# A four-layer attention and feed-forward kernel on one core: projections chunk by chunk in the opening, kept copies behind the linear features, weight splits grouped

## The chip, the cores and the metric

One core of one Trainium2 chip. A time is device microseconds (us) of one execution. Engines: TensorE (PE, with its weight loads PEld), VectorE (DVE), ScalarE (ACT), GpSimd (POOL) and SyncE (SP), which here only issues DMAs. Each engine works through its own list in order; semaphores make one wait for another.

## The reference

`x` is [2, 1024, 128] in float32. Eight sublayers follow, each as `x = x + layernorm(f(layernorm(x)))`:

```python
f0 = causal softmax attention, 16 heads of 8, rotary q and k      # softmax(rope(q) rope(k)^T / sqrt(8)) v, then W_o
f1 = x + 0.5 * mlp(layernorm(x))                                  # 128 -> 512 silu -> 128, dequantised weights
f2 = gated attention: sigmoid(s - mu) * exp(s), normalised        # no mask
f3 = (silu(x @ Wg) * (x @ Wu)) @ Wd                               # 384 wide
f4 = y + mlp(layernorm(y)),  y = x + linear_attention(layernorm(x))   # features elu(.)+1; mlp 128 -> 512 gelu -> 128
f5 = 16 experts of 176, top 4 in 2 of 4 groups, and a shared one
f6 = linear attention
f7 = 8 experts of 512, top 2
```

## The kernel before

The 2048 tokens are 16 tiles of 128, four tiles to a chunk, four chunks (`NC` = 4); chunks 0 and 1 are batch 0. `X` holds the stream, `XN` the normalised tokens, `hT` (in the tensor that the profile calls SHARED) their transpose, `XH` a second copy; PS is the PSUM memory with 8 banks of 512. No scheduler: the block of each engine at the end of the code is its order.

**An edge** joins two sublayers. Per chunk, DVE takes the statistics of the sublayer's output (`dve_y`), POOL forms its reciprocal root (`pool_y`), DVE adds it to `X` and takes the statistics of the sum (`dve_x`), POOL forms scale and bias (`pool_x`), ACT normalises (`act_apply`, L354), PE transposes (`pe_turn_x`, L389), ACT copies the transpose to `hT` (`act_turned`, L365). Edges 1 and 4 have `keep=True`: a feed-forward or linear attention inside the sublayer has a residual of its own, so `dve_keep` (L295) writes the normalised chunk to `XH`, with a root `RSK` from POOL (L341, L342). These copies are read by the first addition of the inner residual (L272 or L286), not earlier.

**Opening.** DVE fills the key buffers with ones (L2388, so that the rows that hold the running maxima are ones) and one PSUM bank with zeros, then takes edge 0's statistics. PE transposes all four chunks, computes the values of all (`pe_values`, L454) and then q, k and their swapped forms of each chunk (`pe_project`, L482, two banks pairs in turn). Of each of the eight pieces (chunk, q or k), DVE forms the rotation (`dve_rope`, L494, L495, L500) in float32, and ACT and POOL split it by turns into three bf16 parts (`act_split_one` L506, L508; `split` L561, L564). Two buffers QF hold the pieces, so a piece is formed only when the one two before is split. When a batch's four pieces are split, SP writes q and k with 6 DMAs each to DRAM (`sp_stack`, L572), waits for all 12, and loads head groups back in the stacked layout (L579). Then the causal attention begins with the maxima of the scores (PE L677, DVE L697).

**Linear attention (f4).** For each of 12 jobs (per chunk one of q, two of k and v), PE multiplies into one of two banks, ACT takes exp, DVE forms the feature (`dve_linear`, L1350, L1351) and so frees the bank. `dve_linear_norm` (L1374 to L1376) divides at the end; `pe_ffn` with edge "4b" is the feed-forward that follows (weights `L2A`, `L2B`).

**First experts (f5).** The products run in float32r with each weight split in a rounded part and its rest. POOL makes these: 15 pieces, `pool_split5(m, k)` for m = gate, up, down and k = 0 to 4, each a cast (L1636) and a subtraction (L1638) of 128x640, in the order of the table `W5`. PE waits with `pe_split5` for the pieces of its next 5 of 25 row blocks, starting with block 4. `pool_rest_of_h` (L1664) does the same with the tokens. Meanwhile DVE works out the routing in four parts, `dve_route5_a` to `d`, for batch 0 ahead of the experts and for batch 1 between them (part a behind the fifth block).

## Time and profile before

| | |
|---|---|
| median of 3 runs | 1683.56 us (1683.44 to 1688.61) |
| the profiled execution | 1686.57 us, span 1684.8 us |
| busy: PE, DVE, ACT, POOL | 1315.4, 1091.3, 1146.9, 265.4 us |
| granted TensorE clock, mean | 0.88 |
| chain that ended last | PE 41%, ACT 24%, DVE 19%, issue 11%, POOL 3% |

The span runs from the first instruction to the last. No engine is busy all the time, so a stage is read by the waits in it. The chain is followed back from the last instruction: a microsecond taken out of a place that it passes through can shorten the whole.

### The profile page before, as it was taken

The page shows a single profiled execution, that of the slowest core. Times are in us where ns is not written, and L with a number is a line of the kernel's source. Part 1 is how long each engine was busy: PE and PEld are TensorE (multiplying, and loading weights), DVE is VectorE, ACT ScalarE, POOL GpSimd, SP SyncE. Part 2 cuts the span into 40 slices and gives each one's busy share as a digit, 9 for nine tenths or more (in the row PEclk, how much of TensorE's full clock was granted, in tenths as well). Part 3 has the DMA queues.
Part 4 walks back from the last instruction along what each step waited for, and adds up shares of the span by engine and source line. Part 5 has one row for each costly group of instructions (what it writes and reads, how often), then busy time and mean ns, then how long its engine had stood idle before and what let it go on. Part 6 is the DMA issues. An engine that isn't in the chain of part 4 may idle for free.

```text
span 1684.8 us, 22199 instructions
## 1 busy us (share of the span) xinstructions
PE 1315.4 (78%) x8121; PEld 660.7 (39%) x8156; DVE 1091.3 (65%) x2049; ACT 1146.9 (68%) x1619; POOL 265.4 (16%) x373
## 2 busy tenths in 40 slices
PE   5388898875777777777777785787999888787996
PEld 3133333343111111111111244565666666565774
DVE  5687877154446645755754855478766777666887
ACT  3147777755999999999999543453465455777885
POOL 3500003041000000000000232451101024612000
PEclk9579999997687887887788797978999999899998
DMA  3702020003310110000100400000000002000000
GB/s 113 206 3 40 22 40 3 2 1 99 88 19 0 20 19 1 20 19 0 19 1 0 166 1 0 1 1 1 1 0 1 1 13 94 1 1 1 6 8 13
DMA packets 22604, 44.07 MB, mean 26 GB/s; under 512 B 3232, under 2 KB 7584, under 8 KB 21728
## 3 DMA queue, kind: packets, MB, share of 16 engines
q1 hardware_dynamic: 22496, 42.66, 9.0%
q8 instruction: 64, 1.05, 0.3%
q14 instruction: 44, 0.36, 0.1%
HBM read 28.89 MB, written 13.76 MB: 25 GB/s over the span
## 4 chain that ended last, share of the span: by engine, by line
PE 41%; ACT 24%; DVE 19%; issue 11%; POOL 3%; SPq 1%; DMA 1%; ACTq 0%; POOLq 0%; DVEq 0%
ACT SHARED L999 14%; PE PS L1669 5%; PE PS L1671 4%; PE PS L1670 4%; PE PS L956 4%; PE PS L788 4%; PE PS L943 3%; DVE NM L697 3%; PE PS L610 2%; DVE SHARED L1009 2%; PE PS L677 2%; PE PS L752 2%; DVE ROUNDED L1806 2%; ACT SHARED L768 1%; ACT XN L354 1%
## 5 line engine op out<-in xcount | busy, mean ns | idle before, releaser
L999 ACT ACTIVATE SHARED<-PS 128x1536 f32<-128x1536 f32 (+1 forms) x352 | 466.1, 1437 | 31.2 <-PE PS L943 30.2
L943 PE MATMUL PS<-QS,KS 51*128 51x512 bf16 (+1 forms) x1024 | 242.0, 461 | 134.2 <-ACT SHARED L999 128.8
L1009 DVE TENSOR_TENSOR SHARED<-SHARED 128x1536 f32<-128x1536 f32 (+1 forms) x176 | 286.6, 1705 | 86.7 <-ACT SHARED L999 86.7
L1669 PE MATMUL PS<-ROUNDED 128*128 128x512 f32 x556 | 251.3, 452 | 28.6 <-DVE ROUNDED L1806 10.9
L768 ACT ACTIVATE SHARED<-PS 128x512 f32<-128x512 f32 (+3 forms) x384 | 164.3, 494 | 102.7 <-PE PS L756 92.6
L1671 PE MATMUL PS<-ROUNDED 128*128 128x512 f32 x556 | 224.1, 403 | 0.0
L1670 PE MATMUL PS<-ROUNDED 128*128 128x512 f32 x556 | 223.4, 402 | 0.0
L943 PEld LDWEIGHTS PS<-QS,KS 51*128 51x128 bf16 (+1 forms) x1024 | 41.2, 99 | 386.8 <-ACT SHARED L999 358.7
L956 PE MATMUL PS<-SHARED,Vg 128*16 128x512 f32 x1024 | 157.9, 694 | 1.7 <-DVE SHARED L1009 1.6
L697 DVE TENSOR_REDUCE NM<-PS 128x2 f32<-128x1024 f32 (+3 forms) x128 | 128.9, 1022 | 38.6 <-PE PS L683 30.5
L1669 PEld LDWEIGHTS PS<-ROUNDED 128*128 128x128 f32 x556 | 110.0, 198 | 53.9 <-DVE ROUNDED L1806 14.2
L1770 ACT ACTIVATE KS<-PS 128x512 f32<-128x512 f32 x100 | 59.7, 597 | 101.2 <-PE PS L1671 101.1
L1671 PEld LDWEIGHTS PS<-ROUNDED 128*128 128x128 f32 x556 | 108.2, 195 | 25.3
L1670 PEld LDWEIGHTS PS<-ROUNDED 128*128 128x128 f32 x556 | 109.1, 196 | 20.7 <-issue 0.5
L323 POOL TENSOR_SCALAR VEY<-MVY 128x4 f32<-128x4 f32 x32 | 7.6, 236 | 637.6 <-DVE MVY L265 636.8
L468 POOL COPY Vg<-XH 128x256 f32<-128x256 f32 x16 | 6.3, 400 | 630.0 <-PE PS L956 396.9
L2148 DVE TENSOR_TENSOR ROUNDED<-KS,ROUNDED 128x512 fp32r<-128x512 f32 x103 | 76.5, 747 | 44.4 <-ACT ROUNDED L2079 43.2
L677 PE MATMUL PS<-SHARED 48*128 48x512 bf16 (+3 forms) x384 | 70.3, 365 | 40.1 <-DVE NM L697 18.4
L788 PE MATMUL PS<-SHARED,Vg 128*16 128x256 f32 (+3 forms) x1152 | 92.0, 392 | 11.1 <-ACT SHARED L768 9.6
L2073 ACT ACTIVATE KS<-PS,C 128x512 f32<-128x512 f32 x103 | 71.0, 689 | 42.6 <-PE PS L1671 42.3
L1817 DVE TENSOR_TENSOR SHARED<-KS,PS 128x512 f32<-128x512 f32 x88 | 60.2, 684 | 56.1 <-ACT KS L1770 50.4
L1758 ACT ACTIVATE ROUNDED<-KS 128x512 fp32r<-128x512 f32 x100 | 62.9, 629 | 42.0 <-DVE KS L1824 41.6
(275 smaller groups left out, 2035.6 us busy)
## 6 DMA issues: line engine op xcount, KB each, us to landing
qx<-SHARED SPq DMA_DIRECT2D x24, 256.0 KB, 3.8
kx<-SHARED SPq DMA_DIRECT2D x24, 256.0 KB, 3.9
SHARED<-in_moe SPq DMA_DIRECT2D x3, 1600.0 KB, 13.4
SHARED<-qx SPq DMA_DIRECT2D x16, 192.0 KB, 4.6
SHARED<-kx SPq DMA_DIRECT2D x16, 192.0 KB, 5.2
QS<-qx SPq DMA_DIRECT2D x16, 192.0 KB, 4.6
KS<-kx SPq DMA_DIRECT2D x16, 192.0 KB, 5.0
W<-in_w SPq DMA_DIRECT2D x1, 1152.0 KB, 7.6
```

Source lines behind the costliest of these rows:

```text
L677: ins = pe.matmul(PS[:, slot(k, x):slot(k, x) + n], q[r, p, qt * P:qt * P + P], key[r, p, hi * CH:hi * CH + n], start=True, stop=not diag)
L697: dve.tensor_reduce(out=dst, in_=src, axis=AX.X, op=ALU.max, negate=True).then_inc(A[0, "a_red"], 1)
L768: act.activation(PB[t % 3][:, h, q0:CH], bank(RING0[n % 3], q0), ACT.Exp, scale=SCORE_SCALE)\
L788: ins = pe.matmul(PS[32 * h:32 * h + VC, 6 * CH + a:6 * CH + b], Vg[g % 2][:, kt, h, :], PB[t % 3][:, h, a:b], start=kt == 0, stop=last an ...
L943: ins = pe.matmul(bank((v % 2) * GRP + f - a), KS[g % 2][r, h // 2, kt * P:kt * P + P], QS[g % 2][r, h // 2, qh * CH:(qh + 1) * CH], start ...
L956: ins = pe.matmul(PS[32 * h:32 * h + VC, 6 * CH:7 * CH], Vg[g % 2][:, kt, h, :], EX[:, f * CH:f * CH + CH], start=kt == 0, stop=kt == KT - 1)
L999: act.activation(dst, PS[:, (v % 2) * GRP * CH:((v % 2) * GRP + b - a) * CH], ACT.Exp if second == qh else ACT.Sigmoid, scale=SCORE_SCALE)\
L1009: dve.tensor_tensor(ex_tile(j), ex_tile(j), GR[w % RING][:, 0:(b - a) * CH], ALU.mult)\
L1669: pe.matmul(dst, w[0], x[0], start=start, stop=False)
L1670: pe.matmul(dst, w[0], x[1], start=False, stop=False)
L1671: return pe.matmul(dst, w[1], x[0], start=False, stop=stop)
L2148: dve.tensor_tensor(HL7[k], GE7[k], HG7[k].bitcast(F32), ALU.subtract).then_inc(A[7, "lo"], 1)
```

## The change

- **Kept copies.** `dve_keep` no longer stands in the edge's loop; at edge 1 all 16 tile copies follow the edge, at edge 4 they follow all of `dve_linear`. POOL forms the roots of all 16 tiles in two instructions behind the edge (`pool_keep`).
- **Opening.** The key buffers' ones move behind the first four rotations; the PSUM fill is dropped. PE projects chunk 0 as soon as chunks 0 and 1 are transposed, each piece with a signal of its own, and the values come last. ACT issues the 6 DMAs of k of batch 0.
- **Splits.** All POOL splits leave their places between the edges; 11 of 15 stand between edges "4b" and 5, and 4 behind the routing. `L2A` and `L2B` get other places in the arena, since the down weights are now split while that feed-forward runs.

```diff
         def dve_keep(dve, own, e, c):
-            dve.wait_ge(k_root, e.n_keep(c))
+            dve.wait_ge(k_root, e.n_keep(NC - 1) // NC)
             for t in tiles(c):
...
-            for s in range(NC + 2):
+            for s in range(NC + 1):
                 if s < NC:
...
                     dve_x(dve, own, e, s - 1)
-                if e.keep and 0 <= s - 2 < NC:
-                    dve_keep(dve, own, e, s - 2)
+            for c in range(NC if e.keep else 0):
+                dve_keep(dve, own, e, c)
...
                 pool.tensor_tensor(NBX[:, k], NMX[:, k], RSX[:, k], ALU.mult).then_inc(x_scale, 1)
-            if e.keep:
-                own.link(pool.tensor_scalar(VEK[:, k], MVX[:, k, 1], 1.0, EPS, ALU.mult, ALU.add))
-                pool.tensor_tensor(RSK[:, k], VEK[:, k], ROOT[:, k], ALU.pow).then_inc(k_root, 1)
+
+        def pool_keep(own):
+
+            pool = own.eng
+            own.link(pool.tensor_scalar(VEK[:, :], MVX[:, :, 1], 1.0, EPS, ALU.mult, ALU.add))
+            pool.tensor_tensor(RSK[:, :], VEK[:, :], ROOT[:, :], ALU.pow).then_inc(k_root, 1)
...
                     pool_x(own, e, s - 1)
+            if e.keep:
+                pool_keep(own)
...
-        def pe_project(pe, L, mats):
-
+        def qkv0_bank(c, m):
+
+            return bank((4, 0)[c % 2] + m)
+
+        def pe_qkv0(pe):
+
+            pe_turn_x(pe, edges[0], 0)
+            pe_turn_x(pe, edges[0], 1)
+            pe.wait_ge(w_in, 16)
             for c in range(NC):
-                if c == 1:
-                    pe.wait_ge(A[L, "vall"], NC)
-                if c >= 2:
-                    pe.wait_ge(A[L, "qf"], 2 * (c - 1))
-                for m, name in enumerate(mats):
-                    ins = pe.matmul(bank(4 * (c % 2) + m), W[:, WM[name], :], chunk(hT, c),
-                                    start=True, stop=True)
-                ins.then_inc(A[L, "proj"], 1)
-
-        def dve_rope(dve, L):
-
-            for i in range(2 * NC):
+                if c == 0:
+                    pe.wait_ge(h_ready, 1)
+                elif c == 1:
+                    pe_turn_x(pe, edges[0], 2)
+                    pe_turn_x(pe, edges[0], 3)
+                    pe.wait_ge(h_ready, NC)
+                else:
+                    pe.wait_ge(A[0, "qf"], 2 * (c - 1))
+                for m, name in enumerate(("q0", "qs0", "k0", "ks0")):
+                    ins = pe.matmul(qkv0_bank(c, m), W[:, WM[name], :], chunk(hT, c), start=True, stop=True)
+                    if m % 2:
+                        ins.then_inc(A[0, "proj"], 1)
+            pe.wait_ge(A[0, "qf"], 2 * (NC - 1))
+            for c in range(NC):
+                pe_values(pe, 0, c, None)
+            pe.wait_ge(A[0, "qf"], 2 * NC)
+
+        def dve_rope(dve, L, i0, i1):
+
+            for i in range(i0, i1):
                 c, m = divmod(i, 2)
                 pos = slice((c % QH) * CH, (c % QH) * CH + CH)
-                dve.wait_ge(A[L, "proj"], c + 1)
+                dve.wait_ge(A[L, "proj"], i + 1)
                 if i:
                     dve.wait_ge(A[L, "qf"], i)
-                dve.tensor_tensor(TA, bank(4 * (c % 2) + 2 * m), COS[:, pos], ALU.mult)
-                dve.tensor_tensor(TB, bank(4 * (c % 2) + 2 * m + 1), SIN[:, pos], ALU.mult)\
+                dve.tensor_tensor(TA, qkv0_bank(c, 2 * m), COS[:, pos], ALU.mult)
+                dve.tensor_tensor(TB, qkv0_bank(c, 2 * m + 1), SIN[:, pos], ALU.mult)\
                    .then_inc(A[L, "rope"], 1)
...
-        def act_split(act, L):
-            for i in range(2 * NC):
+        def act_split(act, L, b):
+            for i in range(2 * QH * b, 2 * QH * b + 2 * QH):
                 act_split_one(act, L, i)
...
+        def stack(eng, L, b, m):
+
+            dst, parts = ((qx, Q_PART), (kx, K_PART))[m]
+            eng.wait_ge(A[L, "part2"], 2 * QH * (b + 1))
+            for t, part in enumerate(parts):
+                eng.dma_start(dst[b * H:(b + 1) * H, t * HD:(t + 1) * HD, :],
+                              PARTS[:, m, part, b * S:(b + 1) * S]).then_inc(A[L, "q_wr"], 16)
+
+        def stacked(sp, L, b):
+            sp.wait_ge(A[L, "q_wr"], 16 * 2 * TERMS * (b + 1))
+
+        def act_stack0(act):
+            stack(act, 0, 0, 1)
+
         def sp_stack(sp, L, b):
-            sp.wait_ge(A[L, "part2"], 2 * QH * (b + 1))
-            for m, (dst, parts) in enumerate(((qx, Q_PART), (kx, K_PART))):
-                for t, part in enumerate(parts):
-                    sp.dma_start(dst[b * H:(b + 1) * H, t * HD:(t + 1) * HD, :],
-                                 PARTS[:, m, part, b * S:(b + 1) * S]).then_inc(A[L, "q_wr"], 16)
-            sp.wait_ge(A[L, "q_wr"], 16 * 2 * TERMS * (b + 1))
+            stack(sp, L, b, 0)
+            if (L, b) != (0, 0):
+                stack(sp, L, b, 1)
+            stacked(sp, L, b)
...
                     if s == 0:
+                        pe.wait_ge(A[0, "vall"], NC)
                         pe.wait_ge(A[0, f"m_ld{g % 3}"], 32 * (g // 3 + 1))
...
         LF = arena(1152, 1152)
-        L2A = arena(2304, 512)
-        L2B = arena(2816, 512)
+        L2A = arena(22720, 512)
+        L2B = arena(32256, 512)
         R2W = arena(3328, E2)
...
                     ((LI, l1int),),
-                    ((arena(2304, 1024), l2fc), (arena(3328, 48), r2w), (arena(3376, H + D), r2b)),
+                    ((L2A, l2fc[:, 0:512]), (L2B, l2fc[:, 512:1024]), (arena(3328, 48), r2w), (arena(3376, H + D), r2b)),
                     ((MG, moe2[0]), (MU, moe2[1]), (MD, moe2[2]), (SEL2, moe2sel.bitcast(BF16))))):
...
         SHARED5 = 3
-        W5 = {(m, k): n for n, (m, k) in enumerate([("g", 4), ("u", 4), ("g", 0), ("u", 0), ("g", 1), ("u", 1),
-                                                    ("g", 2), ("u", 2), ("d", 4), ("d", 0), ("d", 1),
-                                                    ("g", 3), ("u", 3), ("d", 2), ("d", 3)])}
+        SPLITS5 = [("g", 4), ("u", 4), ("d", 4), ("g", 0), ("u", 0), ("d", 0), ("g", 1), ("u", 1), ("d", 1),
+                   ("g", 2), ("u", 2), ("d", 2), ("g", 3), ("u", 3), ("d", 3)]
+        EARLY5 = 11
+        W5 = {piece: n for n, piece in enumerate(SPLITS5)}
...
             pool_edge(pw, edges[3])
+            pool_edge(pw, edges[4])
+            pool_edge(pw, edges["4b"])
             late(pool, 2)
-            pool_split5(pool, "g", 4)
-            pool_split5(pool, "u", 4)
-            pool_edge(pw, edges[4])
-            pool_split5(pool, "g", 0)
-            pool_split5(pool, "u", 0)
-            pool_edge(pw, edges["4b"])
-            pool_split5(pool, "g", 1)
-            pool_split5(pool, "u", 1)
-            pool_split5(pool, "g", 2)
-            pool_split5(pool, "u", 2)
+            for m, k in SPLITS5[0:EARLY5]:
+                pool_split5(pool, m, k)
             pool_edge(pw, edges[5])
...
             pool.wait_ge(A[5, "cw"], 1)
-            pool.wait_ge(y_ready, YB[5])
-            pool_split5(pool, "d", 4)
-            pool_split5(pool, "d", 0)
-            pool_rest_of_h(pool, 5, 1)
-            pool_split5(pool, "d", 1)
-            pool_split5(pool, "g", 3)
-            pool_split5(pool, "u", 3)
-            pool_split5(pool, "d", 2)
-            pool_split5(pool, "d", 3)
-            pool_rest_of_h(pool, 5, 2)
-            pool_rest_of_h(pool, 5, 3)
+            for m, k in SPLITS5[EARLY5:]:
+                pool_split5(pool, m, k)
+            for c in range(1, NC):
+                pool_rest_of_h(pool, 5, c)
             pool_from_moe5(pool, pw)
...
-            pe_edge(pe, edges[0])
-            pe.wait_ge(w_in, 16)
-            pe.wait_ge(c_in, 48)
-            pe.wait_ge(v_own, 1)
-            pe.wait_ge(h_ready, turned(0))
-            for c in range(NC):
-                pe_values(pe, 0, c, None)
-            pe_project(pe, 0, ("q0", "qs0", "k0", "ks0"))
-            pe.wait_ge(A[0, "qf"], 2 * NC)
+            pe_qkv0(pe)
             pe_attend0(pe)
...
             act.wait_ge(c_in, 48)
+            act_split(act, 0, 0)
+            act_stack0(act)
+            act_split(act, 0, 1)
             for c in range(NC):
                 act_values(act, 0, c)
-            act_split(act, 0)
             act_attend0(act)
...
+            dve_edge(dve, own, edges[0])
+            dve.wait_ge(rope_in, 32)
+            dve_rope(dve, 0, 0, 2 * QH)
             dve.memset(K0_ALL, 1.0).then_inc(A[0, "ones"], 1)
-            own.link(dve.memset(bank(6), 0.0))
-
-            dve_edge(dve, own, edges[0])
+            dve_rope(dve, 0, 2 * QH, 2 * NC)
             dve.wait_ge(c_in, 48)
             dve_mu_rows(dve, own)
-            dve.wait_ge(rope_in, 32)
-            dve_rope(dve, 0)
             dve_attend0(dve)
...
             late(dve, 1)
-            dve_edge(dve, own, edges[4], lambda c: dve_glu(dve, c + 1) if c + 1 < NC else None)
+            e4 = edges[4]
+            for c in range(NC):
+                if c + 1 < NC:
+                    dve_glu(dve, c + 1)
+                dve_y(dve, own, e4, c)
+                if c:
+                    dve_x(dve, own, e4, c - 1)
+            dve_x(dve, own, e4, NC - 1)
             for c in range(NC):
                 dve_linear(dve, own, c)
+            for c in range(NC):
+                dve_keep(dve, own, e4, c)
             dve_linear_norm(dve, own, 0)
```

TensorE's order in the opening, before (L389 transposes, L454 values, L482 projections, L677 and L683 the first scores):

```order
L389 MATMUL PS<-ident,XN 128x128 x16
L454 MATMUL PS<-W,SHARED 128x128 x16
L482 MATMUL PS<-SHARED,W 128x512 x16
L677 MATMUL PS<-SHARED 128x128 x2
L683 MATMUL PS<-masks 128x64 x4
```

and in the changed kernel (L394, L498, L459 and L709, L715 are the same five):

```order
L394 MATMUL PS<-ident,XN 128x128 x8
L498 MATMUL PS<-SHARED,W 128x512 x4
L394 MATMUL PS<-ident,XN 128x128 x8
L498 MATMUL PS<-SHARED,W 128x512 x12
L459 MATMUL PS<-W,SHARED 128x128 x16
L709 MATMUL PS<-SHARED 128x128 x2
```

The first four projections now stand between the transposes of chunks 1 and 2, and the values moved from ahead of all projections to behind them.

VectorE's order where edge 4 ends and the features begin, before (L280 to L265 are `dve_x`, L295 the kept copies, L1350 and L1351 the features):

```order
L295 TENSOR_SCALAR XH<-X,MVX,RSK 128x128 x4
L280 SCALAR_TENSOR_TENSOR X<-PS,RSY,X 128x128 x4
L262 BN_STATS STX<-X 128x6 x4
L265 BN_AGGR MVX<-STX 128x2 x4
L295 TENSOR_SCALAR XH<-X,MVX,RSK 128x128 x8
L1350 TENSOR_SCALAR SHARED<-SHARED 128x512
L1351 SCALAR_TENSOR_TENSOR SHARED<-PS,SHARED 128x512
L1350 TENSOR_SCALAR SHARED<-SHARED 128x2x128
```

and in the changed kernel (L1383 and L1384 are the features):

```order
L280 SCALAR_TENSOR_TENSOR X<-PS,RSY,X 128x128 x4
L262 BN_STATS STX<-X 128x6 x4
L265 BN_AGGR MVX<-STX 128x2 x4
L1383 TENSOR_SCALAR SHARED<-SHARED 128x512
L1384 SCALAR_TENSOR_TENSOR SHARED<-PS,SHARED 128x512
```

and, at the end of its features, ahead of `dve_linear_norm` (L1407 to L1409):

```order
L1383 TENSOR_SCALAR SHARED<-SHARED 128x2x128
L1384 SCALAR_TENSOR_TENSOR SHARED<-PS,SHARED 128x256
L295 TENSOR_SCALAR XH<-X,MVX,RSK 128x128 x16
L1407 TENSOR_SCALAR SHARED<-PS 128x32
L1408 RECIPROCAL SHARED<-SHARED 128x32
L1409 TENSOR_TENSOR XN<-PS,SHARED 128x256
```

The 16 kept copies moved from ahead of the first feature to between the last feature and the first division.

## Rows read from the trace of the kernel before

**Rows 1.** Timeline of the opening: start us, us, engine, line, operation [idle before <- releaser].

```profile
2.07 5.18 DVE L2388 MEMSET SHARED<- 128x6144 bf16 x1 [2.07 <-issue]
...
7.87 0.87 DVE L262 BATCH_NORM_STATS2 STX<-X 128x6 f32<-128x128 f32 x4
...
14.85 1.12 PE L389 MATMUL PS<-ident,XN 128*128 128x128 f32 x4 [0.69 <-ACT XN L354]
...
20.04 0.60 ACT L365 ACTIVATE SHARED<-PS 128x512 f32<-128x512 f32 x1 [0.72 <-PE PS L389]
...
20.78 5.97 PE L454 MATMUL PS<-W,SHARED 128*128 128x128 f32 x32 [0.78 <-ACT SHARED L365]
...
26.59 7.03 PE L482 MATMUL PS<-SHARED,W 128*128 128x512 f32 x16
...
32.35 0.63 ACT L506 ACTIVATE SHARED<-SHARED 128x512 bf16<-128x512 f32 x1 [4.96 <-DVE SHARED L500]
...
39.35 1.56 DVE L500 TENSOR_TENSOR SHARED<-SHARED 128x512 f32<-128x512 f32 x1
...
44.23 1.16 POOL L564 TENSOR_TENSOR SHARED<-SHARED 128x512 bf16<-128x512 f32 x1 [0.81 <-ACT SHARED L508]
```

**Rows 2.** The opening's loads of X and of the rotary tables, issue to landing.

```profile
L2228 SPq DMA_DIRECT2D X<-in_x x4: 445/494/507, 0.7 to 2.3; - x4
...
DMA to landing us min/median/max: 3.0/3.7/4.7
...
SHARED<-in_rope SPq DMA_DIRECT2D x2, 512.0 KB, 8.2
```

**Rows 3.** Timeline, from the stacking of batch 0 to the first score.

```profile
45.42 3.85 SPq L572 DMA_DIRECT2D qx<-SHARED  x6
...
63.47 0.29 PE L677 MATMUL PS<-SHARED 48*128 48x128 bf16 x2 [17.11 <-DMA SHARED<-kx]
```

**Rows 4.** Windows: start:end, length, busy us by engine, granted clock, DMA share, GB/s.

```profile
53.00:55.00 2.00, 0.00 (x0) 0.00 (x0) 0.19 (x1) 0.85 (x2) 1.55 (x2) 0.50 0.97 316
```

**Rows 5.** One instruction line over the whole program: GpSimd's two large opening memsets.

```profile
L2259 POOL MEMSET Vg<- x2: 311/312/312, 1.8 to 2.2; 128x256 f32 x2
```

**Rows 6.** Chain that ended last, before the first feed-forward: start us, us, what.

```profile
341.94 1.01 POOL RSK L342
```

**Rows 7.** Timeline around the start and end of the linear attention's features.

```profile
1009.68 1.12 DVE L280 SCALAR_TENSOR_TENSOR X<-PS,RSY,X 128x128 f32<-128x128 f32 x4
...
1012.41 1.11 DVE L295 TENSOR_SCALAR XH<-X,MVX,RSK 128x128 f32<-128x128 f32 x4 [0.29 <-POOL RSK L342]
...
1015.58 0.72 POOL L1636 CAST ROUNDED<-SHARED 128x640 fp32r<-128x640 f32 x1
...
1015.65 4.61 DVE L295 TENSOR_SCALAR XH<-X,MVX,RSK 128x128 f32<-128x128 f32 x4 [2.13 <-POOL RSK L342]
...
1020.18 0.41 DVE L1350 TENSOR_SCALAR SHARED<-SHARED 128x512 f32<-128x512 f32 x1
...
1045.53 0.19 DVE L1374 TENSOR_SCALAR SHARED<-PS 128x32 f32<-128x32 f32 x1 [0.85 <-PE PS L1292]
```

**Rows 8.** Timeline of the second feed-forward: GpSimd's splits and norms, ScalarE's normalising.

```profile
1070.73 1.53 POOL L1638 TENSOR_TENSOR ROUNDED<-SHARED,ROUNDED 128x640 fp32r<-128x640 f32 x1
...
1084.57 0.19 POOL L323 TENSOR_SCALAR VEY<-MVY 128x4 f32<-128x4 f32 x1 [5.48 <-DVE MVY L265]
...
1107.02 1.65 ACT L354 ACTIVATE XN<-X,NBX,RSX 128x128 f32<-128x128 f32 x4 [7.40 <-POOL NBX L339]
```

**Rows 9.** Timeline of the first experts' start.

```profile
1115.20 0.22 DVE L1569 TENSOR_TENSOR SHARED<-SHARED 128x64 f32<-128x64 f32 x1
...
1124.00 0.72 POOL L1636 CAST ROUNDED<-SHARED 128x640 fp32r<-128x640 f32 x1 [9.19 <-DVE SHARED L1500]
...
1137.20 1.48 DVE L1569 TENSOR_TENSOR SHARED<-SHARED 128x64 f32<-128x64 f32 x1
...
1143.10 2.48 POOL L1664 TENSOR_TENSOR ROUNDED<-XH,ROUNDED 128x512 fp32r<-128x512 f32 x2
```

More of the change, by code:

```diff
@@ L1106, in sandwich @@
         f0_in = sem("f0_in")
-        N_LATE = (1, 3, 4, 2, 3, 2)
+        N_LATE = (1, 4, 4, 2, 3, 2)
         late_in = [sem(f"late_in{i}") for i in range(len(N_LATE))]
```

## The prediction

> **What bounds the kernel now.** I read the page, then the chain that ended last, then the timeline of every place that the diff touches. The long parts (both softmax-like attentions, the experts) are the same instructions before and after. What can change is how early each starts, so I look only at the joints, and there only at what the chain passes through.
>
> In the opening [rows 1] DVE writes ones for 5.18 us, then zeros, and takes its first statistics at 7.87, though X's first load is issued at 0.7 and lands some 3 us later [rows 2]. PE's last transposed chunk is copied by ACT at 20.04 (0.60 long), then the values run 5.97 us, and only then the projections (7.03 us for two chunks). The first split begins at 32.35, and batch 0's fourth piece is split at 44.23 + 1.16 = 45.39. I call this moment T. From 32.35 to T is one loop between ACT and POOL, 13.04 us, which nothing else feeds or stops. The loads of the first head group end at 63.47, when PE takes its first score [rows 3]; T to there is 18.08.
>
> In the linear attention [rows 7] the last statistics start at about 1010.8, and the first feature at 1020.18. Between stands a kept copy of 4.61 us for four tiles, beside POOL's split that starts at 1015.58. The POOL roots for these copies are also in POOL's way at the edge before the first feed-forward [rows 6]. And when the first experts start, DVE's routing of batch 1 runs into POOL's splits [rows 9].
>
> **Opening.** Without the two fills DVE's statistics start when X is there, 0.7 + 3.0 = 3.7, so 4.1 us earlier than 7.87; the later chunks arrive 4.7 us after issue at the latest, ahead of their turn. POOL and ACT of edge 0 follow in step, 4.1 us earlier. PE finishes the second chunk's transposes at 14.85 + 1.12 - 4.1 = 11.9 (the first chunk's copy is done by then, and W as well) and projects chunk 0 in 7.03/2 = 3.5, to 15.4. Then it transposes chunks 2 and 3 (1.1 each), and ACT, which waits for these, ends its edge with two copies of 0.6: 15.4 + 1.1 + 1.1 + 0.7 = 18.3. The first rotation cannot start before the tables land, at 6.5 + 8.2 = 14.7 [rows 2]; three DVE operations of 0.7 later, at 16.9, its piece is there, so ACT's 18.3 decides. T becomes 18.3 + 13.0 = 31.3: **14.1 us earlier**.
>
> From T to the first score I take the same 18.1. Twelve DMAs now start from two engines, and that could save at most SP's second half of issuing, some 4 us. But the window shows the 16 DMA engines 97% busy [rows 4], so the bytes decide, and I take 0. Two waits are new and must fit into these 18.1. The ones must be written before SP may load: they start after the fourth rotation, which ended at 39.35 + 1.56 = T - 4.5, and end at T + 0.7. Hidden, with 10 us to spare. Then PE: its values now wait for the sixth rotation and its first score for the eighth. The sixth comes at about T + 5 (ones to T + 0.7, then two rotations of 2.1). The values take 5.97 at the high clock level (2.4 GHz) and 11.9 at the low one (1.2), which gives T + 17 at worst, 1 us ahead of the data. The eighth: ACT first issues six DMAs (0.65 each, to T + 3.9), then its four pieces take 13.0; the last rotation is one and a half pieces ahead of the end, T + 12.5. So the first score still waits for the data. SP's stacking of batch 1 can start at T + 16.9, where it also started before, behind 12 loads. Bounds of this part: 14 + 4 = 18 if the second queue helped after all, and 14 - 5 = 9 if the fill stalls POOL (a rival below).
>
> **Edge 1.** The root for the kept copy sits on the chain, 1.01 + 0.19 for its partner [rows 6]; it now comes behind everything. 1.2 us gained. The 16 copies (16 x 0.28 = 4.4) fall into DVE's wait for the feed-forward. Bounds 0 to 1.5.
>
> **Linear attention.** Ahead of the features DVE sheds all four copy groups. The last chunk's `dve_x` began at 1009.68 behind two of them, 1.11 each; without these, and with POOL's roots gone from between, it begins at 1007.5 and ends 2.4 later: first feature at 1010.0. ACT's exp for it is ready by 1009.9 in the trace of before. So 1020.18 moves by 10.1. The copies now stand between the last feature and the first division, which before waited only 0.85 [rows 7]. POOL is idle there, so 16 copies cost 4.4, and the path grows by 4.4 - 0.85 = 3.55. Net 6.55. PE stands idle ahead of the features for 15 us now and for 5 then. While it stands the granted clock goes to its low level (0.50 with PE at 0.00 busy [rows 4]), and the first 7 us of work behind such a stop are slow. If the shorter stop spares the clock, up to 2.4 more are gained; I take 0. Bounds 5.5 to 9. **6.5 us.**
>
> **Splits.** One costs 0.75 + 1.53 = 2.28, so 11 cost 25.1 us and run from 1069.9 to 1095.0 on before's clock [rows 8]. Edge 5's first POOL norm is asked for at 1084.57 and now waits for 10.4 us. Behind it queue POOL's second norm and DVE's `dve_x` of chunk 0, and ACT's first normalising. With the splits done at 1095.0, these end at 1096.3, 1098.9 and 1102.6, and ACT's next work stands at 1107.02, set by chunk 2's products. So nothing is lost, and there are 2 us of slack before the third chunk's norm would be late.
>
> At the experts POOL starts at 1124.00 as before, with 4 splits and 3 remainders instead of 7 and 3. At the contended rate of 2.8 per split it ends at about 1124 + 11.2 + 3.8 = 1139, where it ended at 1143.10 + 2.48 = 1145.6 before. DVE's eight small operations of part a take 7.5 us from 1136.9 (one of them 1.48 instead of 0.22 [rows 9]) and PE stops for them. With POOL gone after the first one or two, they take 2 to 3. Gain 5; bounds 2 and 8 (with the clock, that fell in this stop). **5 us.**
>
> **Sum.** 14.1 + 1.2 + 6.5 + 5 = 26.8. Against the profiled execution's 1686.57 that gives 1659.8; that execution is 3.0 above the median, so against the median 1683.56 I expect 1656.8.
>
> **The rivals.**
>
> *The fill of ones stalls POOL.* It now runs beside the last three POOL operations of batch 0's splits; if it holds something that they need, T comes up to 5.2 later, gain 21.6, time 1662. For it: DVE and POOL clearly block each other (the kept copy's 4.61, the rotation's 1.56 where the first one took 0.69). Against it: during the same fill in the opening POOL's memset of 256 took 0.312 as the one before it, 0.311 [rows 5]. But that one only writes, so it proves little for operations that read. Chance 12%. The Trainium skill (SBUF — State Buffer, Who interferes with whom) says that the port pair shared by VectorE and GpSimd is an exclusive lock for the whole instruction, for copies and tensor_scalar in fast modes and for operations with two SBUF inputs; for this chip it does not name memset, and by that the time would stay 1657.
>
> *Less idleness, higher clock.* PE's stops in all three joints get shorter, and the values run just ahead of the maxima, whose phase ran at the low level. Shorter scores on the chain there could give 3, the features 2.4, the experts 2: gain 34, time 1650. Chance 20%.
>
> *PE is late for the first score.* The values would have to take more than 13 us; each microsecond more is lost. With 5 lost the time is 1662. Chance 8%.
>
> *The copies cost more than they free.* If the 16 copies ran at the contended rate, 4.61 per four, they would take 18 and turn the linear part into a loss of 8; time 1671. It needs POOL to work during them, and POOL has nothing to do until edge "4b". Chance 3%.
>
> *Slower than before: edge 5 behind the splits.* Every microsecond by which the 11 splits end after 1097 delays the experts. It decides once they eat the other gains: 2 + 27 us late, which is 54 for 11, or 4.9 per split, twice what any split took. At 2.8 the loss would be only 4. Chance 2%, at about 1690.
>
> *Within 0.3% (5 us), that is nothing told from no change by a measurement of this kernel:* the opening's gain given back in the causal attention, by a later transfer, together with a loss at the copies. Chance 2%.
>
> **How the numbers follow.** Main forecast 53%, its own range 1651 to 1662. The clock case reaches down to 1648, the two cases at 1662 up to 1667 with the bounds of the opening. Outside 1648 to 1667 I leave the rest. Faster by more than 0.3%: 96%; same 2%; slower 2%.
>
> **What would show it.** First DVE statistics near 3.8; the first split near 18.3 and the first score near 49.4, waiting for kx; POOL operations of 1.15 during the fill. First feature near 10 us behind its last statistics' POOL root of before, right behind `dve_x` of chunk 3; 16 copies in 4.4 us with PE idle behind them. Eleven splits in 25 us, ACT's work at edge 5 unmoved against the feed-forward's end. Part a of the batch-1 routing in 2 to 3 us. It would be wrong if PE were the last one awaited at the first score, or if a shared transfer or the clock made an unchanged stage longer.

## The result, and the profile after

| us | before | changed |
|---|---|---|
| first set, median (runs) | 1684.13 (4: 1683.44 to 1688.61) | 1667.95 (4: 1671.35, 1659.85, 1664.82, 1671.09) |
| the same kernel again, three sets | 1685.26 (23), 1683.90 (9), 1688.84 (11) | 1655.57 (6), 1657.16 (5), 1656.94 (5) |
| all runs (before: with the profiled 1686.57) | 1686.3 (48) | 1657.4 (20: 1653.73 to 1671.35) |

The first set's ratio is 0.9891 [0.9848, 0.9935], the three repeats' 0.9823 [0.979, 0.9856], 0.9839 [0.9813, 0.9866] and 0.9805 [0.9782, 0.9828]. The first median lies 1 us above my range of 1648 to 1667, all three others within 1.3 us of the forecast. The work of this document is to say why both are true of one kernel.

The profiled execution of the first set is its slowest (1671.35, span 1669.5). Timeline of its opening, to be held against [rows 1, 3, 5]:

```profile
3.83 0.87 DVE L262 BATCH_NORM_STATS2 STX<-X 128x6 f32<-128x128 f32 x4 [3.83 <-DMA X<-in_x]
...
11.72 6.13 PE L498 MATMUL PS<-SHARED,W 128*128 128x512 f32 x8
...
18.33 1.09 ACT L370 ACTIVATE SHARED<-PS 128x512 f32<-128x512 f32 x2 [3.53 <-PE PS L394]
19.30 0.63 ACT L526 ACTIVATE SHARED<-SHARED 128x512 bf16<-128x512 f32 x1
...
29.10 5.18 DVE L2406 MEMSET SHARED<- 128x6144 bf16 x1 [1.23 <-issue]
29.24 1.15 POOL L581 TENSOR_TENSOR SHARED<-SHARED 128x512 f32<-128x512 f32 x1
...
32.38 6.97 SPq L592 DMA_DIRECT2D qx<-SHARED  x6
32.38 6.85 ACTq L592 DMA_DIRECT2D kx<-SHARED  x6
38.32 6.59 PE L459 MATMUL PS<-W,SHARED 128*128 128x128 f32 x32 [6.70 <-DVE SHARED L520]
39.28 0.63 ACT L526 ACTIVATE SHARED<-SHARED 128x512 bf16<-128x512 f32 x1 [8.22 <-issue]
...
50.80 0.29 PE L709 MATMUL PS<-SHARED 48*128 48x128 bf16 x2 [5.89 <-DMA SHARED<-kx]
```

The statistics start when X lands. The four projections of chunk 0 (eight matmuls in the trace) take 6.1 us, the first ones 0.85 us each; in [rows 1] 16 took 7.03, 0.44 each. The first split stands at 19.30 (32.35 before), T, the moment at which batch 0's pieces are all split, is 32.35 (45.39), and the first score comes at 50.80, still waiting for kx: 12.7 us earlier. POOL's 1.15 beside the fill of ones is its length without it. The same kernel around the linear attention and the second feed-forward, against [rows 7, 8]:

```profile
1008.30 0.40 DVE L1383 TENSOR_SCALAR SHARED<-SHARED 128x512 f32<-128x512 f32 x1
...
1032.26 4.19 DVE L295 TENSOR_SCALAR XH<-X,MVX,RSK 128x128 f32<-128x128 f32 x16
...
1036.36 0.18 DVE L1407 TENSOR_SCALAR SHARED<-PS 128x32 f32<-128x32 f32 x1
1037.54 2.38 PE L1325 MATMUL PS<-SHARED 128*128 128x144 f32 x8 [3.89 <-DVE XN L1409]
...
1060.09 0.72 POOL L1669 CAST ROUNDED<-SHARED 128x640 fp32r<-128x640 f32 x1
...
1083.71 1.54 POOL L1671 TENSOR_TENSOR ROUNDED<-SHARED,ROUNDED 128x640 fp32r<-128x640 f32 x1
1085.33 0.20 POOL L323 TENSOR_SCALAR VEY<-MVY 128x4 f32<-128x4 f32 x1
```

L1383 is the first feature, L1407 the first division, and the eleven splits run from 1060.09 to 1085.25. Before, the first products behind the division took 0.73 and 0.76 us for four each, at the high level of the clock; here the same eight take 2.38, in a low stretch (1034.0 to 1040.8):

```profile
1046.71 0.73 PE L1292 MATMUL PS<-SHARED 128*128 128x144 f32 x4 [0.73 <-DVE XN L1376]
1047.77 0.76 PE L1292 MATMUL PS<-SHARED 128*128 128x144 f32 x4 [0.33 <-DVE XN L1376]
```

And the routing of batch 1 at the experts' start in the changed kernel, against [rows 9]:

```profile
1124.88 0.79 DVE L1599 TENSOR_TENSOR SHARED<-SHARED 128x128 f32<-128x128 f32 x1
1125.70 1.20 DVE L1602 TENSOR_TENSOR SHARED<-SHARED 128x64 f32<-128x64 f32 x1
1126.82 1.31 DVE L1603 TENSOR_TENSOR SHARED<-SHARED 128x64 f32<-128x64 f32 x1
1128.16 0.19 DVE L1604 TENSOR_TENSOR SHARED<-SHARED 128x32 f32<-128x32 f32 x1
```

The way to find lost time between two executions is to take one instruction of each engine in both and subtract its starts, stage after stage. That lead over the kernel before (its profiled execution) is, for the first set's execution, for the first repeat's (1653.73), and for the three parts of the change alone (below):

| lead at (time before) | first set | repeat | opening alone | copies alone | splits alone |
|---|---|---|---|---|---|
| first score, 63.5 | 12.7 | 12.4 | 13.9 | 0.0 | -0.3 |
| end of the causal attention, 334 | 3.7 | 13.7 | 15.2 | 1.3 | -0.1 |
| first feed-forward, 361 | 3.4 | 14.0 | 15.2 | 2.1 | -0.1 |
| end of the gated attention, 949 | 1.7 | 12.8 | 15.2 | 1.5 | 0.1 |
| first feature, 1020.2 | 11.9 | 23.0 | 15.1 | 11.7 | 3.6 |
| second feed-forward, 1082 | 10.7 | 21.8 | 15.2 | 10.3 | 3.5 |
| first experts under way, 1160 | 17.2 | 28.3 | 15.3 | 10.9 | 9.9 |
| end, 1684.7 | 15.2 | 32.8 | 18.2 | 14.7 | 9.9 |

In the first set's execution the joints gave all that was forecast, 12.7 + 9.0 + 6.5, and between the first score and the end of the gated attention 11 us went lost, 9 of them in the causal attention, which the change doesn't touch. The last 4.5 us of the repeat's 32.8 lie behind 1160, where nothing is changed either: the kernel before stood at the low clock level for 30.7 us between 1160 and 1500, the repeat for 17.1. Windows of the first set's execution: most of the causal attention, what came ahead of the first fall of the clock, and places of the loss (columns as in [rows 4]):

```profile
115.00:325.00 210.00, 187.86 (x2482) 77.33 (x2483) 135.74 (x195) 149.22 (x351) 16.82 (x9) 0.94 0.10 21
...
184.00:187.40 3.40, 2.78 (x28) 1.17 (x29) 3.24 (x5) 2.76 (x7) 0.00 (x0) 1.00 0.00 0
187.50:190.90 3.40, 3.40 (x23) 0.85 (x23) 1.00 (x2) 1.28 (x3) 0.00 (x0) 0.50 0.00 0
...
307.00:317.20 10.20, 9.72 (x80) 3.42 (x80) 1.48 (x4) 5.14 (x13) 0.00 (x0) 0.50 0.01 2
```

and of the repeat:

```profile
115.00:325.00 210.00, 184.33 (x2530) 81.20 (x2526) 139.08 (x218) 151.11 (x354) 19.26 (x13) 1.00 0.10 20
...
187.50:190.90 3.40, 3.06 (x49) 1.35 (x45) 2.81 (x3) 2.36 (x6) 0.00 (x0) 1.00 0.00 0
...
307.00:317.20 10.20, 8.12 (x96) 2.68 (x92) 0.08 (x1) 7.90 (x18) 0.00 (x0) 1.00 0.01 2
```

The granted clock fell to 0.50 (1.2 GHz) five times between 187 and 317 us in the one and not at all in the other (whose next low stretch starts at 326.6). At each of the first four falls the lead shrinks by 1.3 to 1.4 us, and by 3.6 at the 10 us one; 1.1 more go near 95 us, where the low stretch of the opening ends 4 us later in the work than before's, and 1.1 come back at a low stretch of before. Ahead of the first fall PE was busy and had then waited 0.58 us for ACT's exp. It waits 0.58 us there once in every head group: of the five such waits between 157 and 280 us the last four, 30.9 us apart, have a fall within 0.7 us of their start, the first has none, and in the repeat none of the five has.

### The profile page after: what moved, and what is told of

The parts are those of the page before. It is cut to its first block and busy times, and to the rows that moved or that the text cites. A ratio compares the mean times of both kernels' runs of the same rounds, so it can differ in the third digit from the quotient of the medians.

```text
span 1669.5 us, 22185 instructions
## 1 busy us (share of the span) xinstructions
PE 1328.5 (80%) x8121; PEld 665.2 (40%) x8156; DVE 1080.4 (65%) x2048; ACT 1147.0 (69%) x1619; POOL 262.6 (16%) x361
## 5 line engine op out<-in xcount | busy, mean ns | idle before, releaser
L1703 PE MATMUL PS<-ROUNDED 128*128 128x512 f32 x556 | 252.5, 454 | 26.8 <-DVE ROUNDED L1840 9.3
L729 DVE TENSOR_REDUCE NM<-PS 128x2 f32<-128x1024 f32 (+3 forms) x128 | 129.1, 1022 | 28.8 <-PE PS L715 20.5
L820 PE MATMUL PS<-SHARED,Vg 128*16 128x256 f32 (+3 forms) x1152 | 97.6, 413 | 11.1 <-ACT SHARED L800 9.6
L2182 DVE TENSOR_TENSOR ROUNDED<-KS,ROUNDED 128x512 fp32r<-128x512 f32 x103 | 76.6, 747 | 44.9 <-ACT ROUNDED L2113 43.8
L709 PE MATMUL PS<-SHARED 48*128 48x512 bf16 (+3 forms) x384 | 72.2, 375 | 28.5 <-DVE NM L729 17.9
```

The source lines that it names most:

```text
L729: dve.tensor_reduce(out=dst, in_=src, axis=AX.X, op=ALU.max, negate=True).then_inc(A[0, "a_red"], 1)
L820: ins = pe.matmul(PS[32 * h:32 * h + VC, 6 * CH + a:6 * CH + b], Vg[g % 2][:, kt, h, :], PB[t % 3][:, h, a:b], start=kt == 0, stop=last an ...
L1703: pe.matmul(dst, w[0], x[0], start=start, stop=False)
L2182: dve.tensor_tensor(HL7[k], GE7[k], HG7[k].bitcast(F32), ALU.subtract).then_inc(A[7, "lo"], 1)
```

## The experiments

**The three parts alone.** The opening's hunks on the kernel before; the kept copies' hunks (in both edges, with the single root); the splits' hunks (order, number of early ones, the two weight tiles' new place).

> The opening's part of the change alone, everything behind it as before. In the profiled execution of the changed kernel the first score came 12.67 us earlier than before, of which 1.7 were left at the end of the first half of attention: 9 stretches of 3.41 us at a granted clock of 0.50 between 187 and 317 us stood against two before. Theory 1 (the loss is one of granted clock and differs between executions of the same program): the first score is again 12.7 us earlier, and the times spread over some 8 us; median 1671 to 1678, fastest near 1671. Theory 2 (the shifted opening always costs the causal attention its clock or some wait): what is left is 2 to 5 us in every execution, 1679 to 1682, with a spread as before (5 us).

> Only the kept copies moved (and their roots in one go behind the edge), in edges 1 and 4; opening and splits as before. From the changed kernel's profile: first feature 10.2 us earlier, copies 4.2 us in the path of the normalization behind it, 2.6 us back from a low-clock stretch that fell elsewhere. If these belong to this part, 8.0 to 9.5 us less: 1674 to 1676. If the part of it at the first feature came from the splits taken out of POOL's stream ahead of edge 4, less than 5 us: above 1678. My prediction had put 6.5 us on it.

> Only the weight splits moved into the feed-forward (with the place of two weight tiles), the rest as before. The changed kernel gained 6.5 us between the end of the feed-forward and the first expert's second product; my prediction had 5 (2 to 8). Expected 1676 to 1679. If the splits matter to edge 4 too (POOL free for its roots), more, down to 1672; if the 11 splits are late for edge 5 without the 10 us that the linear attention gives, nothing or a loss: 1683 to 1690.

Measured against 1685.26 in one set: opening 1670.61 (0.9898 [0.9868, 0.9929]), copies 1681.09 (0.996 [0.9938, 0.9982], runs from 1671.82 to 1688.06), splits 1677.57 (0.9944 [0.9922, 0.9967]). The parts make 14.65 + 4.17 + 7.69 = 26.5, the whole 29.7 in this set. The opening keeps its 13.9 through the causal attention, and its five runs (1668.33 to 1674.87) all lie below the 1679 to 1682 of the theory that shifting it costs, which refutes that theory. The splits came out as expected. The copies' median, 4.2 less, lies where I had put the case that the gain at the first feature comes from the splits. But its spread is wide, and its profiled execution, the fastest, has the 10.2 at the first feature without them, and 8.8 behind the copies, where the whole change has 10.2 and 9.0.

One overlap shows in the table: the splits alone already bring 3.5 us at the first feature, a gain that the copies alone bring too. By the leads up to the second feed-forward the two parts therefore make 3.2 us more than the whole (8.8 + 3.4 against 9.0), while by the medians all three make 3.2 less; the spread of the copies' runs is wider than either, so the medians don't settle how the parts add. Timeline of the kept copies of the last chunk in the kernel with the splits alone moved away; [rows 7] have the same four with a split beside them, at 4.61:

```profile
1015.58 1.12 DVE L295 TENSOR_SCALAR XH<-X,MVX,RSK 128x128 f32<-128x128 f32 x4 [2.14 <-POOL RSK L342]
```

**The changed kernel again, three times**, unedited.

> The changed kernel again, unedited. Theory 1 (granted clock differs between executions): the profile shows other low stretches in the causal attention than the nine short ones seen, the times again spread from about 1660 to 1671, and the time goes with the number of low stretches ahead of 320 us. Theory 2 (the loss belongs to the change): the same stretches at 187, 218, 249, 280 and 307 us again in this profile.

> The changed kernel once more, as the base of this call and for its spread: the first set had a median of 1667.95 us with two of four runs at 1671, the second 1655.57 with four of six below 1657. If the granted clock of the execution makes it, the times follow the mean clock as there (0.887 at 1653.7, 0.882 at 1659.9, 0.879 at 1664.5, 0.874 at 1671.2), 1.35 us for each 0.001.

> The changed kernel again, as the base of this call: 1654 to 1660 us median, by the granted clock of its executions.

Medians 1655.57, 1657.16, 1656.94. Over all 20 runs the time follows the mean granted clock that comes with each: 0.885 to 0.887 at 1653.7 to 1656.4, 0.883 to 0.885 at 1656.9 to 1658.7, 0.882 at 1659.8 (both), 0.879 to 0.880 at 1664.2 to 1665.1, 0.874 at 1671.1 and 1671.4. Of the profiles, the first repeat's has no low stretch from 115 to 325 us, that of the second (1665.14 us) has four, at 126, 157, 277 and 304 to 314 us, and that of the third (1656.37 us) three, at 186, 217 and 248 us: its lead falls from 13.6 at the first score to 9.6 at the end of the causal attention. So these stretches differ between executions of one program, and the loss goes with them. The kernel before spreads likewise, 1682.21 (0.885) to 1698.44 (0.873).

**k's writes back on SyncE.**

```diff
             act_split(act, 0, 0)
-            act_stack0(act)
             act_split(act, 0, 1)
...
-            if (L, b) != (0, 0):
-                stack(sp, L, b, 1)
+            stack(sp, L, b, 1)
```

> The changed kernel, with the six writes of k for batch 0 issued by SyncE behind those of q, as before the change, and none by ScalarE. With two queues the twelve issues took 6.9 us (1.15 each on either engine), and ScalarE's next split stood 8.25 us. My prediction: the second queue gains nothing, since the 16 DMA engines are 97 % busy; first score within 0.5 us, ScalarE's splits of batch 1 end 5 to 6 us earlier (near 45 us), the time the same within 1 us. Rival (the issues bound the transfers after all): twelve issues at 0.65 end at 7.8 us in place of 6.9, the loads and the first score come 1 us later, the time 1 us longer.

1656.67 against 1657.16 of the changed kernel in the same set: no difference. Timeline:

```profile
31.70 3.86 SPq L592 DMA_DIRECT2D qx<-SHARED  x6
35.60 5.01 SPq L592 DMA_DIRECT2D kx<-SHARED  x6
43.72 0.34 SPq L610 DMA_DIRECT2D SHARED<-qx  x1
...
35.49 0.63 ACT L526 ACTIVATE SHARED<-SHARED 128x512 bf16<-128x512 f32 x1 [5.12 <-DVE SHARED L520]
...
50.57 0.29 PE L708 MATMUL PS<-SHARED 48*128 48x128 bf16 x2 [6.42 <-DMA SHARED<-kx]
```

From the first write's issue to the first load's is 12.0 us with one queue and 11.5 and 12.4 in two executions with two; to the first score it is 18.9, against 18.4 and 19.1. (From T it is 18.1 to 19.1 in all ten profiles with two queues, 18.9 in this one and 18.1 before.) Issuing by two saved 2 us of issue (8.9 to 6.9) and nothing on the path. The Trainium skill (DMA: Bandwidth & Descriptors, Issuing engines are not separate DMA queues) says that several issuing engines save only the sequencer's time to initiate; these numbers agree. ACT's next split came 3.4 us earlier than in the first repeat, and so did the end of batch 1's splits, 48.5, not 5 to 6: the split then waits for the rotation behind the fill of ones. The time shows that nothing waits for that either.

**Kept copies by chunk.**

```diff
             for c in range(NC):
                 dve_linear(dve, own, c)
-            for c in range(NC):
                 dve_keep(dve, own, e4, c)
```

> The changed kernel, with the kept copies of chunk c behind the features of chunk c, not all 16 behind those of chunk 3. In the repeat of the changed kernel the 16 copies took 4.19 us on VectorE (1021.18 to 1025.4) and took 3.2 to 4.2 us of the lead; VectorE waited 2.98, 1.92 and 2.62 us in front of the first feature of chunks 1 to 3. Theory (copies cost only where nothing is waited for): three groups of 1.1 us fall into those waits, one stays in the path; 3.1 us less than the changed kernel in the same call (2.0 to 3.5). Rival: TensorE waits for the second and third feature of a chunk, and each group of copies delays the next features by its 1.1 us; then no difference.

1652.08 (0.9797 [0.9774, 0.9821]) against 1657.16. Timeline, features and copies in turn, then the first division:

```profile
1001.72 0.29 DVE L1383 TENSOR_SCALAR SHARED<-SHARED 128x256 f32<-128x256 f32 x1 [1.64 <-ACT SHARED L1370]
1003.76 1.12 DVE L295 TENSOR_SCALAR XH<-X,MVX,RSK 128x128 f32<-128x128 f32 x4 [1.28 <-POOL RSK L345]
1005.46 0.43 DVE L1383 TENSOR_SCALAR SHARED<-SHARED 128x512 f32<-128x512 f32 x1 [0.58 <-ACT SHARED L1370]
...
1022.25 1.11 DVE L295 TENSOR_SCALAR XH<-X,MVX,RSK 128x128 f32<-128x128 f32 x4
1023.27 0.19 DVE L1407 TENSOR_SCALAR SHARED<-PS 128x32 f32<-128x32 f32 x1
```

Each of the first three groups falls into a wait for ACT, which shrinks by it (2.98 to 0.58 with the wait for the root in it); the lead over the changed kernel's first repeat grows by 3.25 us in this stage. The forecast was 3.1. The stage also has 3.4 us less of low clock (1024.0 to 1027.4 against 1022.9 to 1029.7), but 3.1 of the 3.25 stand already at the fourth group of copies, at 1022.25 and so ahead of it; 0.2 at most are the clock's. The other 1.9 of the 5.1 between the medians aren't seen in this stage, and no run shows what makes them.

**All 15 splits early.**

```diff
-        EARLY5 = 11
+        EARLY5 = 15
```

> The changed kernel, with all 15 weight splits ahead of edge 5 in place of 11. My prediction gave 11 splits 2 us of room and said that each us past it costs one. Four more take 4 times 2.28, 9.1 us: edge 5 starts 7 to 9 us later, and nothing is left to gain behind it; 6.5 to 9 us more than the changed kernel. Rival (the experts' first products wait for the later splits, not for edge 5): the loss stays below 3 us.

1661.88 against 1657.16, 4.7 more, between my two expectations. The lead over the changed kernel falls by 8.1 us at edge 5 and regains 4.1 at the experts' start. Timeline (second feed-forward, then the start of the routing of batch 1, with its last small operation):

```profile
1087.27 0.19 POOL L323 TENSOR_SCALAR VEY<-MVY 128x4 f32<-128x4 f32 x1
...
1125.47 0.28 DVE L1599 TENSOR_TENSOR SHARED<-SHARED 128x128 f32<-128x128 f32 x1
1125.80 0.23 DVE L1602 TENSOR_TENSOR SHARED<-SHARED 128x64 f32<-128x64 f32 x1
...
1126.85 0.19 DVE L1608 TENSOR_TENSOR SHARED<-SHARED 128x32 f32<-128x32 f32 x1
```

The eight small operations of the routing take 1.6 us with POOL gone, 4.1 in the changed kernel, 7.5 before. So four more splits cost 8.1 of their 9.1 us (1.0 us of room, where I had 2), and the changed kernel still loses 4.1 us at the experts to the four it does there.

**Four splits beside the linear attention, and with the copies by chunk; then eight.** POOL waits for the weights (`late`) and does the first four (eight) pieces ahead of its work for edge "4b", the rest of the 15 behind it. `GAP5` is 4 (8), `EARLY5` is 15, and the order of the pieces is changed so that the first four (eight) are of gate and up.

```diff
+            late(pool, 2)
+            for m, k in SPLITS5[0:GAP5]:
+                pool_split5(pool, m, k)
             pool_edge(pw, edges["4b"])
-            late(pool, 2)
-            for m, k in SPLITS5[0:EARLY5]:
+            for m, k in SPLITS5[GAP5:EARLY5]:
```

> The changed kernel, with four of the 15 weight splits between GpSimd's work for edge 4 and for edge 4b (where it waited 36.7 us with nothing to do, from 1002.7 to 1039.3 us in the repeat of the changed kernel) and the other eleven where its eleven stand, so that all 15 are done ahead of edge 5. With all 15 behind edge 4b, edge 5 came 8.1 us later and the start of the experts won back 4.1 of it. Theory (the experts' start waits for splits that stand behind edge 5): the 4.1 us stay, edge 5 is as in the changed kernel; 3 to 4.5 us less than it. Rival (GpSimd's splits slow VectorE's features beside them, the price that the move out of the linear attention had saved): each of the four 2.28 us splits costs VectorE up to its own length in the path; from 0 to 5 us more than the theory, no gain or a loss.

> Both: kept copies by chunk behind the features, and four splits beside the linear attention, all 15 ahead of edge 5. If they add up, 3.2 and 4.1, 7 us less than the changed kernel: 1648 to 1651. If copies and splits get in each other's way beside the features, between 3 and 6 less.

> The same with eight splits beside the linear attention in place of four (18.2 us of GpSimd's 36.7 idle), seven behind edge 4b. GpSimd is then free 9 us ahead of edge 5. In the changed kernel its eleven splits ended when edge 5 already had its first sums waiting, by about 1 us: 0 to 1.5 us less than with four. Rival (splits beside VectorE's features cost): more than with four, by up to 4 us.

Against 1656.94 of the changed kernel in the same set: 1659.89, 1653.78 and 1663.69. All three missed what I had put first. With four splits the rival holds: the lead over the changed kernel falls by 3.2 us in the features, by 2.5 more by the second feed-forward, with a low clock stretch that the changed kernel doesn't have (1051 to 1058 us), and rises by 3.2 at the experts. With the copies by chunk as well, the 3.2 gained lie at the low end of the "between 3 and 6" of copies and splits in each other's way. With eight, 9.9 us more than with four, it is worse than its rival too (up to 4). Its profile loses 4.8 us in the features, 1.4 by the second feed-forward, regains 3.5 at the experts, and so accounts for 2.7 of the 6.8 by which the median lies above the changed kernel's. Another 4.2 come between 1300 and 1500 us, with 17 us more of low clock; whether that is the edit's isn't shown. Timeline of the first of the three, with three features while POOL splits and one after:

```profile
1012.39 0.79 DVE L1383 TENSOR_SCALAR SHARED<-SHARED 128x512 f32<-128x512 f32 x1 [2.98 <-ACT SHARED L1370]
1014.16 1.36 DVE L1383 TENSOR_SCALAR SHARED<-SHARED 128x256 f32<-128x256 f32 x1 [0.25 <-ACT SHARED L1370]
...
1018.49 1.77 DVE L1383 TENSOR_SCALAR SHARED<-SHARED 128x512 f32<-128x512 f32 x1 [1.79 <-ACT SHARED L1370]
...
1028.48 0.43 DVE L1383 TENSOR_SCALAR SHARED<-SHARED 128x512 f32<-128x512 f32 x1 [2.62 <-ACT SHARED L1370]
```

and of the second, where the copies too stand beside them:

```profile
1000.61 4.61 DVE L295 TENSOR_SCALAR XH<-X,MVX,RSK 128x128 f32<-128x128 f32 x4 [1.22 <-POOL RSK L345]
...
1006.10 0.69 DVE L1384 SCALAR_TENSOR_TENSOR SHARED<-PS,SHARED 128x512 f32<-128x512 f32 x1
...
1010.33 1.10 DVE L295 TENSOR_SCALAR XH<-X,MVX,RSK 128x128 f32<-128x128 f32 x4
```

A group of four copies takes 4.61 beside the splits and 1.10 without. The lowest median of all is that of the kernel with the copies by chunk and the eleven splits left where the change puts them: it beats both kernels, before by the ratio above and the changed one by 5.1 us between medians of one set, of which 3.25 were seen in its stage. The one with four splits beside them stands at the same ratio to before in its own set (0.9796 [0.977, 0.9822]), so no run puts one of the two ahead.

## Why the prediction was right, and where it was off

The forecast of 1656.8 stands within 0.6 us of the median of all 20 runs. That closeness is luck: the gain was 28.8 and not 26.8, and the base 1686.3 over all runs and not the 1683.56 of three, and the two errors cancel. The first set's 1667.95 is 11 us off for the reason that the prediction named last, the clock making an unchanged stage longer, which it had given neither a rival nor room in its range. By the steps:

- **Opening, 14.1:** 12.7 and 12.4, 13.9 with the opening alone, and 12.4 to 14.4 (mean 13.4) over the eleven profiles that have this edit. The step that was short is "projects chunk 0 in 3.5": that is the rate of [rows 1], 0.44 us per matmul, but the first ones take 0.85 here, and the whole took 4.5 to 6.1. It was half hidden by "1.1 + 1.1" for the transposes behind, which took 1.0 together. So the first split, expected at 18.3, came at 17.6 to 19.3, and T, expected at 31.3, at 30.7 to 32.35. T to the first score, taken as 18.1, was 18.1 to 19.1.
- **"I take 0" for the second queue** was right, but the working beside it missed that two queues issue at 1.15 us per DMA, not 0.65: ACT was held until T + 6.9, not T + 3.9, batch 1's splits ended at T + 20, and SP stacked batch 1 at T + 20, not T + 16.9. Nothing waited for it: with one queue they ended at T + 16.9 and the time was the same. PE's values ended at about 44.9, T + 12.6, 6 us ahead of the data.
- **The fill of ones (rival, 12%)** did not stall POOL: 1.15 beside it, as without. The Trainium skill (SBUF — State Buffer, Who interferes with whom) gives the lock to tensor_scalar in fast modes and to operations with two SBUF inputs, and does not name memset for this chip; the traces agree on both sides.
- **Edge 1, 1.2:** 0.9 with the copies alone (1.3 to 2.1 in the table, at an equal amount of low clock), but most of it is lost again between 361 and 500 us, where the gated attention begins: at 500 us 0.2 is left (0.0 to 0.2 in six more profiles with the copies moved, and a loss of 0.9 to 1.9 in the four others). All of these have 3 to 7 us of low clock more than before between 334 and 500 us; the opening alone has as much as before and keeps its lead, 15.2 at both ends. The sum had this term at full size.
- **Linear attention, 6.5:** 9.0. The first feature gained 10.2 (forecast 10.1), and 3.3 of it were gone at the first division (3.55 for the copies). The rest is the clock, taken as 0: before, it stood low from 1011.8 to 1028.8 and from 1059.6 to 1066.4; now from 1010.1 to 1016.9 and from 1034.0 to 1040.8. It gave 0.6 among the features, where I had named up to 2.4, took 1.1 in the products behind the first division (2.38 us for eight), and gave 2.6 in the head of the second feed-forward, where I had nothing. Here the clock goes with the kernel: the low stretch in the head of the second feed-forward stands in the profiles of before, of the opening alone, of the splits alone and of the three kernels with splits beside the features, and in none of the eight others.
- **Splits, 5:** 6.5 (6.4 alone). The eleven took 25.2 us (25.1) and held POOL's first sum of edge 5 until 1085.33, while the feed-forward's lead stayed at 10.7. "2 us of slack" was 1.0. The size is partly luck: the batch-1 routing took 4.1 in place of 7.5, a gain of 3.4 where I had about 5 (2 to 3 in place of 7.5). The other 3.1, which the prediction doesn't have, come ahead of it (1.3, VectorE's subtractions of two SBUF inputs at 0.69 to 1.03 us in place of 1.09 to 1.83) and behind it (1.8, with 3.4 us of low clock in place of 10.2).

The four terms measured, 13.4 + 0.2 + 9.0 + 6.5, make 29.1 and not 26.8; the medians over all runs differ by 28.8, those of the three later sets by 29.7, 26.7 and 31.9. The rival of a higher clock was right in part, by 2.1 us in the linear attention and up to 1.8 at the experts of its 7; the clock over the rest of the program varies more from execution to execution (1653.7 to 1671.4) than the change moves it.

What stays open: why the first set had two of four runs at 1671 and the sixteen later runs none, and what makes the clock fall at one passage of a step and not at the next. Both kernels meet it in the causal attention; no run here shows that the change makes it likelier or rarer there.

## What to carry to other kernels

Before explaining a median of four runs, put the mean granted clock of each run beside its time: here 0.013 of clock was 17.6 us, more than half of the change. Align two profiles instruction by instruction at the joints; a gain that shows at its joint and is lost later, at low clock stretches that other executions don't have, is not a wrong estimate of the edit. Work moved off a wait's path should go into waits of its own engine, chunk by chunk, and not beside GpSimd work that takes its operands from the same memory.

## What the runs showed of the hardware

- An fp32 copy with scale from SBUF to SBUF on VectorE takes longer beside GpSimd's two-input operation of 1.54 us: 4.61 us for four copies in place of 1.10, features of 0.43 as long as 1.77; GpSimd's own stays 1.53 to 1.60 there. Beside VectorE's operations on two SBUF inputs, at the experts' start, both sides stretch: VectorE's 0.69 to as much as 1.83 before, GpSimd's 1.54 to as much as 2.07 in the changed kernel. An operation of VectorE with one input from PSUM and one from SBUF is not touched (0.69 in both cases). Beside VectorE's fill of 5.18 us GpSimd's operations took 1.15, and the fill 5.18, as without.
- Twelve DMA issues took 6.9 us from two engines (1.15 each) and 8.9 from one (0.65 for the first six, 0.84 for the rest).
- TensorE's granted clock fell to 0.50 in the middle of dense work, after a wait of only 0.58 us, in some executions of a program and not in others. Each of the 3.4 us stretches cost 1.3 to 1.4 us in the causal attention. In the gated attention (mean granted clock 0.81 from 600 to 800 us, ACT busy for 187.6 of the 200) every execution had the same 167 us of low clock between 500 and 949, so no run shows what it costs there.
